# Three places for normalised rows, tile-wise stores and an earlier first residual in the second stage of an attention and mixture-of-experts block

## What is computed

```python
sa, ca, ga, sb, cb, gb = chunks of silu(c) @ wmod          # per sequence
h = layernorm(x) * (1 + ca) + sa
x = x + ga * (attention(h) @ w_proj.T + b_proj)            # relu(q), relu(k), no softmax
h = layernorm(x) * (1 + cb) + sb
x = x + gb * experts(h)

# attention: vk = v_pad @ k.T per head; out = vk @ q; out = out[:-1] / (out[-1] + 1e-15)
# experts: r = h * rsqrt(mean(h*h) + 1e-6); logits = r * 512**-0.5 * router_scale @ router_w
#   the two largest logits choose the experts, their softmax shares weigh the outputs
#   expert: (gelu(h @ gate) * (h @ up)) @ down * per_expert_scale
```

## Time and profile before

| | |
|---|---|
| time, three runs | 2183.67, 2186.15 and 2193.63 us; median 2186.15 us |
| profiled execution | 2183.3 us, of which the span from the first to the last instruction is 2181.2 us |
| TensorE busy | 2067.9 us (95% of the span) |
| VectorE busy | 1330.3 us (61%) |
| ScalarE busy | 792.7 us (36%) |
| GpSimd busy | 805.1 us (37%) |
| mean granted TensorE clock | 0.976 |
| stage one, two, three | 0 to about 610 us, to about 1007 us, to the end |

### The profile page before, as it was taken

How to read it: one execution, slowest core, us unless ns; L and a number is a source line. 1 busy time by engine, 2 the same in 40 slices (tenths; PEclk the granted TensorE clock), 3 DMA queues, 4 the chain that set the end, 5 groups by cost and what they waited for, 6 DMA issues and landing times.

```text
span 2181.2 us, 42612 instructions
## 1 busy us (share of the span) xinstructions
PE 2067.9 (95%) x9412; PEld 1621.6 (74%) x9413; DVE 1330.3 (61%) x3192; ACT 792.7 (36%) x1495; POOL 805.1 (37%) x622
## 2 busy tenths in 40 slices
PE   7999999999989999984999999999999999999997
PEld 4888878888846666663788888888888778888885
DVE  7655554555368888873555565656565555565654
ACT  3444434444345665651222222222222222222222
POOL 5676646676415666752111111111111111111111
PEclk9999999999979999996999999999999999999998
DMA  8766555656545675766855558558775975865554
GB/s 275 258 196 207 174 202 169 208 168 207 184 143 199 225 273 217 280 247 202 240 126 129 125 129 240 131 124 242 196 176 126 289 172 129 237 133 125 131 109 79
DMA packets 293820, 404.79 MB, mean 186 GB/s; under 512 B 50648, under 2 KB 188888, under 8 KB 285920
## 3 DMA queue, kind: packets, MB, share of 16 engines
q1 hardware_dynamic: 166016, 258.78, 37.2%
q0 software_dynamic: 30096, 72.12, 16.3%
q10 hardware_dynamic: 97488, 71.77, 10.5%
HBM read 210.57 MB, written 191.98 MB: 185 GB/s over the span
## 4 chain that ended last, share of the span: by engine, by line
PE 78%; DVE 7%; DMA 6%; issue 4%; POOL 1%; ACT 1%; SPq 1%; another core or an unknown queue 1%; ACTq 0%; DVEq 0%; POOLq 0%
PE bank L1824 66%; PE bank L1860 8%; DMA expert_rows<-rows,dest 2%; DMA act_rows<-hact 2%; POOL expert_rows L775 1%; PE bank L1805 1%; DVE onf L1315 1%; DVE lnt L1382 1%; DVE x L1344 1%; PE bank L1945 1%; DMA qb<-q_rows 1%; DVE oh L1436 0%; DMA out_rows<-orow,cur_tok 0%; DMA wbuf<-expert_split 0%
## 5 line engine op out<-in xcount | busy, mean ns | idle before, releaser
L1824 PE MATMUL bank<-wbuf,x_t_hi 128*128 x2168 | 684.0, 397 | 28.7 <-DVE x_t_lo L1670 26.3
L796 POOL DMA_INDIRECT out_rows<-orow,cur_tok x135 | 209.0, 1548 | 967.2 <-DVE orow L1729 788.1
L1824 PEld LDWEIGHTS bank<-wbuf,x_t_hi 128*128 128x128 f32 x2168 | 410.7, 190 | 126.1 <-issue 30.5
L1824 PE MATMUL bank<-wbuf,x_t_lo 128*128 x1084 | 429.6, 396 | 0.0
L1824 PE MATMUL bank<-wbuf,act_t_hi 128*128 x1072 | 338.9, 397 | 10.7 <-DVE act_t_lo L1687 6.8
L1676 DVE TENSOR_TENSOR hact<-bank,gact 128x512 f32<-128x512 f32 x135 | 93.3, 691 | 382.7 <-PE bank L1824 364.2
L1824 PEld LDWEIGHTS bank<-wbuf,act_t_hi 128*128 128x128 f32 x1072 | 203.1, 190 | 60.0 <-issue 12.9
L1824 PEld LDWEIGHTS bank<-wbuf,x_t_lo 128*128 128x128 f32 x1084 | 205.6, 190 | 48.2
L1824 PE MATMUL bank<-wbuf,act_t_lo 128*128 x536 | 212.4, 396 | 0.0
L1060 ACT ACTIVATE x_t_hi<-bank 128x512 fp32r<-128x512 f32 x135 | 80.9, 599 | 295.6 <-PE bank L1824 283.1
L1084 ACT ACTIVATE act_t_hi<-bank 128x512 fp32r<-128x512 f32 x132 | 79.0, 599 | 271.3 <-DMA arow<-act_rows 212.9
(11 more groups left out here) (241 smaller groups left out, 3875.5 us busy)
## 6 DMA issues: line engine op xcount, KB each, us to landing
wbuf<-expert_split SPq DMA_DIRECT2D x24, 1536.0 KB
act_rows<-hact ACTq DMA_DIRECT2D x135, 256.0 KB
xrow<-expert_rows SPq DMA_DIRECT2D x538, 64.0 KB
arow<-act_rows ACTq DMA_DIRECT2D x536, 64.0 KB
expert_split<-split_hi SPq DMA_DIRECT2D x32, 768.0 KB, 3.4
expert_split<-split_lo SPq DMA_DIRECT2D x32, 768.0 KB, 5.9
q_rows<-qf SPq DMA_DIRECT2D x16, 1024.0 KB, 6.8
qb<-q_rows SPq DMA_DIRECT2D x16, 1024.0 KB
```

The costliest lines, as they stand in the source:

```text
L796: pool.indirect_dma_start(out=out, out_offset=bass.IndirectOffsetOnAxis(cur_tok[at][:, 0:1], 0), in_=orow[at % 2][:, :], in_offset=None, c ...
L1824: last = mm(dst, stationary(a, f), moving(b, f), start=(first and k == 0), stop=(k == parts * n - 1))
```

## The change

- `rows` gets a third place, `rows2`, and `dest` a third one; group g uses place `g % 3`. `rows2` takes over the memory of `wproj_f`, which is now a view of it. Before its first use, GpSimd clears the columns behind the row (one small memset in group 1) after TensorE's last read of the projection weights; VectorE waits for the same at its first write (group 2) and for the memset at the first weights (group 3).
- `normed(g, t)` now waits for the scatter of group g - 3.
- The store of `x1` is one DMA for each tile (256 KB), issued when that tile's residual is done, with a semaphore for each tile; `residual(g, t)` waits for the store of tile t of group g - 1. The wait for x stands at tile 0 alone.
- On VectorE `residual(g, 0)` moves ahead of `rms_var(g - 1)`, and `rms_seed_squared(g - 1)` behind `recip(g + 1)`. On ScalarE `off_squared(g, 0)` moves ahead of `rms_seed(g - 1)`.

The diff, with some context left out:

```diff
@@ -139,7 +139,8 @@
     gab = sb(keep, "gab", [P, B, C], F32)
-    wproj_f = sb(keep, "wproj_f", [P, FC, C], F32)
+    rows2 = sb(keep, "rows2", [P, TPG, ROW], F32)
+    wproj_f = rows2[:, :, :].rearrange("p t r -> p (t r)")[:, 0:FC * C].rearrange("p (f n) -> p f n", f=FC)
     ones_f = sb(keep, "ones_f", [P, P], F32)
@@ -213,6 +214,7 @@
     rows = [sb(ph2, f"rows{i}", [P, TPG, ROW], F32) for i in range(2)]
+    rows.append(rows2)
     kvp_f = [[rows[b][:, t, 0:C] for t in range(TPG)] for b in range(B)]
@@ -228,7 +230,7 @@
     rn, rrn = (sb(ph2, f"sum_{i}", [P, TPG], F32) for i in range(2))
-    dest = [sb(ph2, f"dest{i}", [P, 2, TPG], U32) for i in range(2)]
+    dest = [sb(ph2, f"dest{i}", [P, 2, TPG], U32) for i in range(len(rows))]
     cnt, ntl, cend = (sb(ph2, f"cnt_{i}", [P, E], F32) for i in range(3))
@@ -297,7 +299,7 @@
         sem("kvp_ready"), sem("kvp_hi_ready"), sem("kvp_lo_ready"), sem("sel_ready"))
-    s_q2, s_x2, s_x1st = sem("q_back"), sem("x_back"), sem("x1_stored")
+    s_q2, s_x2, s_x1st = sem("q_back"), sem("x_back"), [sem(f"x1_tile{t}_stored") for t in range(TPG)]
     s_den, s_aden, s_rec0, s_dene, s_rec, s_rb, s_on = (
@@ -389,6 +391,9 @@
+    def rows_of(g):
+        return rows[g % len(rows)]
+
     def phase1_over(eng):
@@ -402,7 +407,7 @@
             eng.wait_ge(s_scat[t], SCAT * NG)
-        eng.wait_ge(s_x1st, 16 * NG)
+            eng.wait_ge(s_x1st[t], 16 * NG)
         eng.wait_ge(s_zst, 32)
@@ -526,8 +531,9 @@
                 load_q(g + 2, par)
-            sp.wait_ge(s_x1, TPG * (g + 1))
-            sp.dma_start(group_rows(out, g), x1[:, :, :]).then_inc(s_x1st, 16)
+            for t in range(TPG):
+                sp.wait_ge(s_x1, TPG * g + t + 1)
+                sp.dma_start(out[g * GT + t * P:g * GT + (t + 1) * P, :], x1[:, t, :]).then_inc(s_x1st[t], 16)
             if more:
@@ -759,7 +765,7 @@
                 wait_apart(pool, s_rowm, 2 * g)
-            pool.tensor_copy(rows[par][:, :, TOK_AT].bitcast(I32), tok_no[:, :]).then_inc(s_rowm, 1)
+            pool.tensor_copy(rows_of(g)[:, :, TOK_AT].bitcast(I32), tok_no[:, :]).then_inc(s_rowm, 1)
             wait_apart(pool, s_rowm, 2 * g + 1)
@@ -772,8 +778,8 @@
                 for k in range(2):
-                    pool.indirect_dma_start(out=xs, out_offset=bass.IndirectOffsetOnAxis(dest[par][:, k, t:t + 1], 0),
-                                            in_=rows[par][:, t, :], in_offset=None).then_inc(s_scat[t], 16)
+                    pool.indirect_dma_start(out=xs, out_offset=bass.IndirectOffsetOnAxis(dest[g % len(rows)][:, k, t:t + 1], 0),
+                                            in_=rows_of(g)[:, t, :], in_offset=None).then_inc(s_scat[t], 16)
@@ -781,6 +787,10 @@
                 scatter(g - 1, 1 - par)
+            if g == 1:
+                pool.wait_ge(s_mp, B * HG)
+                pool.memset(rows2[:, :, C:], 0.0).then_inc(s_free, 1)
+                pool.wait_ge(s_free, 3)
             number_rows(g, par)
@@ -956,7 +966,7 @@
                 at_least(act, s_var3, g)
-            act.activation(sq_out[:, :], rows[par][:, t, 0:C], ACT.Square, accum_out=ss[:, t:t + 1]).then_inc(s_sq, 1)
+            act.activation(sq_out[:, :], rows_of(g)[:, t, 0:C], ACT.Square, accum_out=ss[:, t:t + 1]).then_inc(s_sq, 1)
@@ -987,10 +997,9 @@
             before_it, more = g > 0, has(g, 1)
+            off_squared(g, 0)
             if before_it:
                 rms_seed(g - 1)
-            off_squared(g, 0)
-            if before_it:
                 h2t_copy(g - 1, 0)
@@ -1338,9 +1347,9 @@
             dve.wait_ge(s_y, TPG * g + t + 1)
-            dve.wait_ge(s_x2, 16 * (g + 1))
             if t == 0:
-                at_least(dve, s_x1st, 16 * g)
+                dve.wait_ge(s_x2, 16 * (g + 1))
+            at_least(dve, s_x1st[t], 16 * g)
             stt(x1[:, t, :], Y_B[t % 2][:, :], 1.0, xb[par][:, t, :], ALU.mult, ALU.add, accum_out=sum2[:, t:t + 1]).then_inc(s_x1, 1)
@@ -1382,11 +1391,13 @@
         def normed(g, t, par):
-            at_least(dve, s_scat[t], SCAT * (g - 1))
+            at_least(dve, s_scat[t], SCAT * (g - len(rows) + 1))
             turn.after(f"centred{t}")
...
                 turn.after(f"rstd{t // 2}")
-            stt(rows[par][:, t, 0:C], lnt[t % 2][:, :], rstd2[:, t:t + 1], mod_row_of(g, 1), ALU.mult, ALU.add).then_inc(s_h2, 1)
+            if g == len(rows) - 1:
+                dve.wait_ge(s_mp, B * HG)
+            stt(rows_of(g)[:, t, 0:C], lnt[t % 2][:, :], rstd2[:, t:t + 1], mod_row_of(g, 1), ALU.mult, ALU.add).then_inc(s_h2, 1)
@@ -1457,16 +1468,18 @@
-        def weights(par, h=ALL):
+        def weights(g, h=ALL):
             turn.after("renorm_recip")
-            turn.did(tt(rows[par][:, h, W_AT:W_AT + E], wts[:, h, :], rrn[:, h].unsqueeze(2).to_broadcast([P, len(tiles_of(h)), E]), ALU.mult), "weights")
+            if g == len(rows) - 1:
+                dve.wait_ge(s_free, 3)
+            turn.did(tt(rows_of(g)[:, h, W_AT:W_AT + E], wts[:, h, :], rrn[:, h].unsqueeze(2).to_broadcast([P, len(tiles_of(h)), E]), ALU.mult), "weights")
...
             renorm_recip(h)
-            weights(par, h)
+            weights(min(g, NG - 1), h)
@@ -1482,16 +1495,16 @@
-        def destinations(par, h=ALL):
+        def destinations(g, h=ALL):
             turn.after("chosen")
             with nc.allow_low_precision("row numbers under 2 ** 24, whole in both types"):
-                dve.tensor_reduce(dest[par][:, :, h], chosen[:, :, h, :], AX.X, ALU.add).then_inc(s_dest, 1)
+                dve.tensor_reduce(dest[g % len(rows)][:, :, h], chosen[:, :, h, :], AX.X, ALU.add).then_inc(s_dest, 1)
...
             places_chosen(h)
-            destinations(par, h)
+            destinations(min(g, NG - 1), h)
@@ -1506,14 +1519,13 @@
             turn.begin(g, ROUTE_STEPS if router else 0)
+            residual(g, 0, par)
             if router:
                 rms_var(g - 1)
-            residual(g, 0, par)
-            if router:
-                rms_seed_squared(g - 1)
             if not last:
...
             if router:
+                rms_seed_squared(g - 1)
                 rms_seed_error()
@@ -1563,11 +1575,11 @@
             if now:
-                weights(1 - par)
+                weights(g - 1)
             seed_error(1)
...
                 next_places()
-                destinations(1 - par)
+                destinations(g - 1)
             rstd2_of(1)
@@ -1990,7 +2002,7 @@
             for f in range(FC):
-                last = pe.transpose(H2_B[t % 2][:, f * P:(f + 1) * P], rows[par][:, t, f * P:(f + 1) * P], ident[:, :])
+                last = pe.transpose(H2_B[t % 2][:, f * P:(f + 1) * P], rows_of(g)[:, t, f * P:(f + 1) * P], ident[:, :])
             last.then_inc(s_h2t, 1)
```

## The result

| | before | after |
|---|---|---|
| median | 2185.35 us (4 runs) | 2230.07 us (2226.41 to 2237.67, 4 runs) |
| ratio | | 1.020, 95% interval 1.018 to 1.022 |
| profiled execution | 2183.3 us | 2237.67 us, span 2235.8 us |

The account below looks back on a forecast made before the run. Stage two was taken as bound by a loop of waits over `rec`, 20.84 us when quiet. Twelve loops at 20.40 gain 12.3, the loop ahead 0.69, together 13.0: 2170.3 profiled, 2173 us median, range 2166 to 2180.

Parts of the forecast that it names:

- 0.25 foreseen: On VectorE, the wait of `rms_var` for ScalarE's last square was to fall from 0.94 to about 0.25 us.
- 0.69 foreseen: On VectorE, `rec` was to come 0.69 us earlier, because the first residual runs inside the wait of `rms_var`.
- the idle time ahead of `spread`: TensorE's idle 0.51 us before `spread` in a quiet loop, said to end on `rec` and go to about 0.
- the two lengths of the earlier trace: GpSimd's eight scatter issues took 10.64 us, or 10.04 in another group; the forecast took a train between them.
- TensorE alone: its own loop without the idle 0.51 is 20.33: One of three loops competing to bind stage two next: TensorE's own, 20.33 us long without its idle time.
- the 7.10: Stretch from the start of `spread` on TensorE (919.02) to the next mark (926.12), part of the 20.84 us loop.
- quiet loop of before: An undisturbed stage-two loop of the kernel before, 905.28 to 926.12, taking 20.84 us; the 12-loop average was 21.43.
- 0.54 <-remote: In a quiet loop `residual(g, 2)` on VectorE waits 0.54 us, read as TensorE being later anyway.
- the prediction's third loop: GpSimd with VectorE: mask, `dest`, scatter train, row numbers and `low_on`, 20.56 us, or 19.96 with the shorter train.
- Slower: the scatter train under VectorE: Rival, chance 0.06: VectorE work under every scatter issue lengthens the train to 14.04 and the loop to 23.96; 2216.5 us.
- The idle time only moves: Rival, chance 0.25: what follows takes back the 0.69, quiet loops stay at 20.84, disturbed ones become quiet; 2179 us.
- The clock, which I expected to rise to 1.00: Sign named for the changed profile: granted clock in the window of stage-two loops rises from 0.99 to 1.00.

Follow-up runs that it names:

- e9: The changed kernel with x1 stored at once for each group, as before, instead of by tiles: ratio 0.999 to the kernel before.
- e1: The changed kernel with the old order on VectorE and ScalarE, third place and stores by tiles kept: ratio 0.998 to the kernel before.
- e2: The kernel before with the new order on VectorE and ScalarE alone, two places and x1 stored at once: ratio 1.000 to the kernel before.
- e4: The changed kernel with twelve more TensorE products ahead of `logits`, which overwrites their result: 2202.37 us, ratio 1.008 to the kernel before.
- e7: e1 with GpSimd's row numbers written ahead of the scatters: 2187.64 us, ratio 1.000 to the kernel before.
- e10: The changed kernel with two unneeded VectorE copies between first residual and row-scale step, making `rec` late again: ratio 0.998 to the kernel before.
- e8: The changed kernel with scattered rows of 48 bytes instead of 2112, the same eight issues: 2231.1 us, ratio 1.019 to the kernel before.
- e12: e1 with two more scatter issues of 48-byte rows ending each train, ten instead of eight: 2238.66 us, ratio 1.026 to the kernel before.
- e13: e1 with tile 3's two scatter issues taken out of the train and issued a group later: 2207.07 us, ratio 1.011 to the kernel before.
- e14: The whole changed kernel with tile 3's two scatter issues taken out of the train and issued a group later: median 2204.5 us.
- e3: The changed kernel with half of each scatter train, four issues, issued one group later: 2229.08 us, ratio 1.019 to the kernel before.

## Why the prediction was wrong

**The steps that came true.** `normed`'s waits and the store's are gone; `rms_var` waits 0.34 (0.25 foreseen); `rec` comes earlier by 13.68 - 12.85 = 0.83 in group 3 (0.69 foreseen); the idle time ahead of `spread` is 0; the train is 10.40 in a slow loop, between the two lengths of the earlier trace rows.

**The step that failed: "TensorE alone: its own loop without the idle 0.51 is 20.33".** I took the 7.10 from `spread` to the mark for TensorE's work. It isn't. TensorE's timeline of that quiet loop of before goes on thus:

```profile
923.81 0.39 PE L1824 MATMUL bank<-kvp_hi,on_lo 128*128 128x512 f32 x1
924.13 1.06 PE L2002 MATMUL bank<-h2t,rw 128*32 128x512 f32 x8
925.13 1.13 PE L1945 MATMUL bank<-rec,less_sel 32*128 32x512 f32 x4
```

The product is done at 924.20, and the mark is at 926.12: 1.92 of the 7.10 is a late signal. Its release hangs on the train, 11.70 after its start; from a mark to the next train's start are 914.42 - 905.28 = 9.14. 11.70 + 9.14 = 20.84, the same loop, without `rec` in it. The two sums agree because `rec` itself follows the mark. The runs tell them apart: in e9 `rec` moves between 13.3 and 14.2 and undisturbed loops stay at 20.8 to 20.9. "0.54 <-remote" was the sign, and I read past it: the matmul had been over for 1.9.

The kernel after itself shows that TensorE's own loop is not 20.33. From the mark of group 2 (691.43) to that of group 3 (710.28) it takes 18.85 us, at a clock of 1.00. No signal is late there: ScalarE copies tiles 2 and 3 one behind the other, and `residual(2)` starts 9.72 us after the train's start without idle time (GpSimd, ScalarE, VectorE):

```profile
700.56 1.58 POOL L781 DMA_INDIRECT expert_rows<-rows,dest  x1 [3.80 <-DVE dest L1501]
...
706.69 0.96 POOL L781 DMA_INDIRECT expert_rows<-rows,dest  x1 [0.30 <-issue]
```
```profile
707.75 1.06 ACT L973 ACTIVATE h2t<-bank 128x512 f32<-128x512 f32 x2
```
```profile
703.60 0.69 DVE L1317 SCALAR_TENSOR_TENSOR rec<-den,rec 128x512 f32<-128x512 f32 x1
...
710.28 0.68 DVE L1353 SCALAR_TENSOR_TENSOR x<-bank,xb 128x512 f32<-128x512 f32 x1
```

The next train starts at 721.22, 20.66 after this one, behind a mask that ends (717.46) with GpSimd's low parts (717.42). That is near the 20.56 of the prediction's third loop, so with signals on time the loops would hardly have stayed at 18.85.

**What was not priced.** The head start also moves TensorE's transposes and spread against GpSimd's train. With `rec` at its old place the transposes got through: in the quiet loop of before the transposes end 6.8 us after the train's start and their signals are on time by the records of semaphores; in the loop shown above they end at 6.55 and wait. What separates the two: `rec` used to lie over an issue, which took 1.46, and held the issues behind it back by half a microsecond; with `rec` early the fifth issue comes at 800.59 - 795.41 = 5.18 instead of 5.68. I had counted that only as a gain in the train's length. In nine of the traces (before, after, e1, e2, e4, e7 to e10) there are 117 trains of eight issues. In all 73 whose fifth issue starts 5.33 us or more after the first, ScalarE copies tile 3 without idle time; in 41 of the 44 with it at 5.16 to 5.19 ScalarE is idle there, up to 3.6 us. The end of the transposes does not separate them: in e9's train at 932.79 they end 6.04 and 6.47 us after its start, earlier than in the slow loop above, and with the fifth issue at 5.33 nothing waits. Nor does an early `rec`: in the loop of 18.85 above it ends 3.73 us after the train's start, in the slow one 3.82. This is a comparison of trains; no edit moved the fifth issue alone. Shown by edits is that the time of `rec` and of what follows it decides (e10), and that the issues and not their data make signals late (e8, e12).

**The rivals.** "Slower: the scatter train under VectorE" had the side right and the mechanism wrong: the train did not grow. "The idle time only moves" (2179, loops of 20.84) is what e1 comes to: 20.85 in its undisturbed loops, and a profiled execution of 2183.5. The clock, which I expected to rise to 1.00, I treated as something that follows from the rest, not as a cost: behind an idle time of 2.65 us it fell, and by the estimate from e4 that is most of what a slow loop loses.

**The parts.** Third place and stores by tiles (e1) shorten the profiled loops from 21.48 to 21.08. In time e1 is 2% below the kernel after, and 0.2% below the kernel before with an interval that reaches 1.000. The third part adds nothing to that: with one store for the group (e2, e9) its 0.69 goes into the store's wait, and with both others in place it does the harm.

**Open.** What in GpSimd's issuing delays TensorE's signals, and why some signals in the stretch pass. Whether VectorE's and ScalarE's signals are late too: of the 21 that they give between 4 and 11.5 us after the train's start at 795.41 only two have a record, both within 0.01 us of the instruction's end. Whether a shorter train shortens the loop: no train of six was run (e13, e14), and e3's fours got the product's signal out in time and lost time at `rank`'s.

## What to carry to other kernels

Before a wait is counted as an engine's work, lay the end of the last instruction that it waits for beside its release; a difference that is constant against another engine's event is a different loop. When a step is moved, list what else moves with it in time, also on engines that the edit doesn't touch. And a small wait that keeps two engines apart can be worth more than it costs: e10 adds 1.19 us of useless work to each group and is 2% faster than the kernel without it. An idle time, in turn, can cost more than its length, where the clock falls behind it.

## What the runs showed of the hardware that was not expected

- While GpSimd issues a train of eight indirect DMAs, signals of TensorE that fall some 5 us or more after its start can come late by up to 5 us, whether a row has 2112 bytes or 48. The last are released 11.5 to 11.8 us after the start of eight issues and about 14.4 after that of ten, although the issues themselves are over at 10.4 and 13.2. In rows of four issues (e3) one signal 2.4 us after the start came up to 3.3 late.
- In loops with TensorE idle for 2.65 us ahead of `logits` the granted clock was 0.81; with work in that place (e4) it was 1.00.
